# Splitting a batch of keys behind a tile's unpacking instead of ahead of it, with the copies and the store one step later

## The reference

```python
x   = x + xattn(layernorm(x), ctx)      # 1600 tokens, 5776 keys, 512 channels, 16 heads of 32
x   = x + ffn(layernorm(x))

q = quant(x @ Wq + bq) per head;  k = quant(ctx @ Wk + bk) per key and head;  v = quant(ctx @ Wv + bv) per column
attn = softmax(q @ k.T);  attn = round(attn / s) * s with s = max / 255
out  = (attn @ v) @ Wp + bp
```

## Time and profile before

| | before |
|---|---|
| median of 3 runs | 1861.85 us (1861.7 to 1870.55) |
| the profiled execution: its own time, its span | 1868.42 us, 1866.6 us |
| busy share of the span: PE, DVE, ACT, POOL | 88%, 91%, 75%, 76% |
| the 200 steps of attention | about 167 us to 1616 us of the span |
| chain of work that ended last, by engine | DVE 48%, PE 20%, POOL 12%, issue 9%, DMA 6%, ACT 4% |

### The profile page before, as it was taken

How to read it: one execution, slowest core, us unless ns; L and a number is a source line. 1 busy time by engine, 2 the same in 40 slices (tenths; PEclk the granted TensorE clock), 3 DMA queues, 4 the chain that set the end, 5 groups by cost and what they waited for, 6 DMA issues and landing times.

```text
span 1866.6 us, 42192 instructions
## 1 busy us (share of the span) xinstructions
PE 1638.0 (88%) x17032; PEld 1157.2 (62%) x17032; DVE 1694.2 (91%) x2665; ACT 1393.2 (75%) x1362; POOL 1422.8 (76%) x1153
## 2 busy tenths in 40 slices
PE   7997889988888888888888888888889888789998
PEld 6884666666555666655566666555555555467776
DVE  6868999999999999999999999999999999976665
ACT  2446889888988888989888988897788888732222
POOL 1432789989988899989888999898898898752232
PEclk9998999999999999989999999999999999889999
DMA  5677998999999998898998999789888998832221
GB/s 174 211 208 191 193 199 176 172 188 184 171 172 187 194 183 186 172 177 168 188 194 172 190 188 177 150 158 186 171 170 156 206 185 153 177 101 45 66 57 46
DMA packets 851533, 309.98 MB, mean 166 GB/s; under 512 B 784966, under 2 KB 813964, under 8 KB 851212
## 3 DMA queue, kind: packets, MB, share of 16 engines
q1 hardware_dynamic: 851340, 307.29, 80.8%
HBM read 74.26 MB, written 39.59 MB: 61 GB/s over the span
## 4 chain that ended last, share of the span: by engine, by line
DVE 48%; PE 20%; POOL 12%; issue 9%; DMA 6%; ACT 4%; SPq 1%; POOLq 0%; DVEq 0%; ACTq 0%
DVE S L1242 43%; POOL PT L1468 9%; PE PS L847 4%; DMA PP<-Pr 4%; PE PS L714 3%; ACT Pr L1054 2%; PE PS L682 2%; PE PK L884 2%; PE PK L655 2%; PE PK L657 2%; PE PO L657 1%; PE PO L655 1%; DMA XIT<-XI 1%; DVE MJ L1268 1%; PE PO L733 1%
## 5 line engine op out<-in xcount | busy, mean ns | idle before, releaser
L1242 DVE TENSOR_SCALAR_CACHE_REDUCE S<-PS,SQN 128x1536 f32<-128x1536 f32 (+1 forms) x768 | 1284.4, 1713 | 29.5 <-PE PS L714 23.3
L1468 POOL CAST PT<-PP 128x1536 uint16<-128x1536 uint8 (+1 forms) x800 | 1100.6, 1420 | 114.6 <-DMA PP<-Pr 112.6
L1054 ACT ACTIVATE Pr<-S,MS 128x5888 uint8<-128x5888 f32 x200 | 1041.2, 5206 | 171.4 <-DVE MJ L1268 141.9
L714 PE MATMUL PS<-KT,QT 96*128 96x512 bf16 (+1 forms) x2496 | 639.0, 376 | 133.2 <-DVE S L1242 120.2
L733 PEld LDWEIGHTS PO<-VI,PT 128*128 128x128 f16 x9200 | 339.9, 96 | 190.5 <-issue 23.3
L714 PEld LDWEIGHTS PS<-KT,QT 96*128 96x128 bf16 (+1 forms) x2496 | 199.5, 100 | 341.9 <-issue 133.5
L733 PE MATMUL PO<-VI,PT 128*128 128x32 bf16 x9200 | 356.7, 178 | 10.9 <-ACT AO L1008 5.5
L655 PE MATMUL PK<-WG,CT 128*128 128x128 f32 (+1 forms) x1288 | 215.0, 297 | 46.9 <-ACT VV L920 40.5
L657 PE MATMUL PK<-CT,WG 128*128 128x128 f32 (+1 forms) x1288 | 212.4, 294 | 0.0
L655 PEld LDWEIGHTS PK<-WG,CT 128*128 128x128 f32 (+1 forms) x1288 | 169.9, 195 | 53.9 <-issue 52.7
L657 PEld LDWEIGHTS PK<-CT,WG 128*128 128x128 f32 x1288 | 167.5, 193 | 1.7 <-issue 0.6
(11 more groups left out here) (151 smaller groups left out, 1563.0 us busy)
## 6 DMA issues: line engine op xcount, KB each, us to landing
CT<-ctxt SPq DMA_DIRECT2D x180, 256.0 KB, 3.2
k_rows<-KS SPq DMA_DIRECT2D x44, 512.0 KB, 4.0
q_rows<-QS SPq DMA_DIRECT2D x13, 512.0 KB, 4.3
W13F<-w13T SPq DMA_DIRECT2D x12, 352.0 KB, 3.5
PP<-Pr SPq DMA_TRANSPOSE x200, 6.0
XT<-x SPq DMA_DIRECT2D x12, 256.0 KB, 3.3
XR<-x SPq DMA_DIRECT2D x12, 256.0 KB, 3.4
base_rows<-XO SPq DMA_DIRECT2D x12, 256.0 KB, 3.4
```

The costliest lines, as they stand in the source:

```text
L714: last = pe.matmul(PS[n % 2][p0:p0 + r, f:f + w], QT[h % 3][0:PARTS * HD, q0:q0 + r], KT[h % 3][0:PARTS * HD, c * CHUNK + f:c * CHUNK + f ...
L1054: act.activation(Pr[i % 2].rearrange("p t q b -> p t b q"), S[i % 2].rearrange("p (t b q) -> p t b q", b=2, q=P), ACT.Exp, bias=MS[:, i % ...
L1242: v.tensor_scalar(S[i % 2][:, c * CHUNK:c * CHUNK + CW[c]], PS[n % 2][:, 0:CW[c]], neg_step, None, ALU.mult, ALU.min, accum_out=MN[:, i % ...
L1468: gp.tensor_copy(PT[i % 2][:, 2 * t0:2 * t1, :].rearrange("p (t b) q -> p t b q", b=2), PP[i % 2][:, t0:t1, :].bitcast(U8).rearrange("p t ...
```

## The change

`k_parts` of a batch moves on GpSimd from ahead of the unpacking of tile s to behind it (2.95 in place of 2). ScalarE's `k_high` moves from step s+2 to s+3, the store from step s+3 to s+4. The planner reads K_STORE as well, so it lays the pieces of heads anew.

```diff
-K_CAST, K_SPLIT, K_STORE = 1, 2, 3
+K_CAST, K_SPLIT, K_STORE = 1, 3, 4
@@ the list of GpSimd's work
-                    todo += [(step + 1, k_scale, (g, b)), (step + 2, k_parts, (g, b)),
+                    todo += [(step + 1, k_scale, (g, b)), (step + 2.95, k_parts, (g, b)),
                              (end + 5.95 + b * 2 / 3, v_quant, (g, b))]
```

## The result

The changed kernel takes 1869.66 us (median of 21 runs, 1862.54 to 1878.59), the kernel before in the same comparison 1863.81 us (21 runs, 1856.2 to 1871.96). The ratio is 1.0032, 95% interval 1.002 to 1.0044: **slower by 0.3%, some 6 us**. The forecast was 1858 and its range ended at 1868, so both the sign and the range missed. The kernel before had its median at 1861.85 us when the forecast was made and 2 us higher in this comparison; 1868 was 0.33% above the former, so the range ended at about the ratio that was measured. The sign is the larger miss.

What follows compares the result with a forecast made beforehand. VectorE bounds the kernel, busy 1400 of 1443 us from step 0 to 198. Terms 3.0 + 0.5 + 2 x 1.0 − 2 x 0.7 = 4.1 us saved, off the 1861.85 us median, gave 1858; range 1849 to 1868.

Steps and rivals of the forecast that it cites:

- The step that failed: Last batch of groups 1 and 2: its KS overwrite waits for the previous batch's store; 0.7 us lost each, bounds 0 and 2.8.
- Late copies cost nothing ahead of a conversion: ScalarE, seven g=1 batches three steps apart: copies right ahead of the next conversion cost nothing; bound 0.3 us each, 2 in all.
- Step 29: VectorE loses 3.52 us there; an earlier unpacking 22 and transpose 25 take back 3.0 us, bounds 0 and 3.5.
- The copies off steps 52 and 102: ScalarE's high-part copies leave steps where they delay the unit's copies PE awaits: 1.0 us gained each, bounds 0 and 1.5.
- The split out of the gap at (2,0): GpSimd's k_parts there leaves a gap, unpacking 51 starts 1.9 us later; costed at nothing, 1.9 at two places without cover.
- Exponential 131: ScalarE's exponential of tile 131 waited 1.62 us for its transpose; 0.5 us gained, bounds 0 and 1.
- The planner: Pieces of K move by a step or two; 1.5 to 2 us more for SP in some steps, hidden under waits.
- the slower one: Last batch's store lands late, unpackings 41 and 91 up to 4 us later, PE's clock drops again: 1871 us, chance 0.15.
- KD's wait: Sign: GpSimd's 67.1 us wait ahead of KD, for ScalarE's conversion, falls below 15 us.
- The wait ahead of KS: Sign: a new GpSimd wait of 2 to 4 us in batches (1,11) and (2,11), released by the store.
- The stretch: Sign: the attention part, steps 0 to 198, gets 4 us shorter while VectorE's busy time stays 1400 us.
- the group ends: Sign of being wrong: the stretches where a group ends, losing 8.6 and 6.0 us before, lose more than 11 and 9.

Runs made afterwards that it cites:

- the split alone: Kernel before with only GpSimd's k_parts moved behind the unpacking; copies, stores and planner as before: 1858.52 us, 0.9963, and again 1861.47 us, 1.0000.
- set 4: Four variants of late copies and stores on one chip, against the kernel before at 1862.22 us: 1865.8, 1863.84, 1861.87 and 1857.02 us.
- set 3: k_parts moved in all four, copies and stores early or late, planner old or new; kernel before 1862.03 us; ratios 1.0000, 1.0005, 1.0057, 1.0038.
- set 2: Four variants of late batches or new planner on one chip, against the kernel before at 1861.67 us: ratios 0.9986, 1.0020, 1.0026, 1.0029.

## Why the prediction was wrong

**The step that failed** is the last batch's: "That stretch is already led in part by SP's own queue, so not all of it counts; I take 0.7 each, bounds 0 and 2.8." The mechanism was there, at both places, with the store issued at 488.33 (488.2 to 489.5 forecast), KS free at 493.18 (491.2 to 493.5) and unpacking 41 at 493.73 (491.9 to 494.1). What was wrong is what that delay is worth. Only the tile's own path was followed, with the rest taken for covered by SP's queue. Behind the same wait stood the value's cast, whose buffer ScalarE needs ahead of an exponential. That path came last, and PE's clock was halved behind it, which the term did not count. Steps 39 to 47 and 89 to 97 grew by 4.6 and 6.3 us in the pair of profiles. Taking the wait away wins 6 to 7 us in the profiled executions and 2 to 5 by the ratios, where the forecast had 1.4 for both places and at most 5.6. Two experiments show that the wait at KS makes the stall: with batch 10 early, and with the last split later, the stretches are back at 63 to 64 us. That it travels by the value's cast is read from the trace: ScalarE's 2.92 us stand ahead of VQ, and what PE and VectorE wait for behind is ScalarE's. The unpackings follow close: PE could not have begun its product of step 46 more than 0.8 us sooner, since unpacking 42 ended at 505.78. Both experiments free both paths, so no run separates them, and neither path alone can be given the whole price.

**Late copies cost nothing ahead of a conversion** ("by the rows this costs nothing; bound 0.3 each, 2 in all") was wrong as well, within its bound. Steps 10, 20 and 30 each took 7.22 us and take 7.82, 7.83 and 7.71: 1.7 us together by the profiles; the medians can't show so little. They stay at 7.22 wherever those copies are early. ScalarE in the changed kernel at the first of them:

```profile
238.92 0.62 ACT L943 ACTIVATE KS<-KD 128x512 bf16<-128x512 bf16 x1
...
246.50 0.20 ACT L1004 ACTIVATE AO<-PO 128x32 f32<-128x32 f32 x1 [0.70 <-PE PO L733]
246.59 0.62 ACT L926 ACTIVATE KI<-KB 128x512 int8<-128x512 f32 x1
```

The copies stand at a step's end, the exponential behind them starts late, and the conversion of the next batch follows it. A step that is "just filled" has no room for 1.1 us more, whatever the one behind it has.

**Step 29** (3.0 forecast) measures 3.8 in the pair of profiles. But the kernel whose split had not moved takes 6.91 us there too, so the split is not needed for it: the new place of copies and store does it as well, and so does the split alone. Which link of the chain lets it go isn't separated. Whether the medians hold it is open: the split alone has step 29 short and stands at 1.0000 in one set and 0.9963 in another. The kernel before was profiled once, in an execution above its median; whether it loses those 3.5 us in every execution isn't settled. One program had step 29 at 6.92 us in one execution and at 8.01 in another. A term read from one execution was booked against the median in full.

**The copies off steps 52 and 102** (1.0 each) were right for the place; for the kernel no gain is shown. With the first batch's copies alone late, steps 48 to 57 and 98 to 107 take 75.4 and 75.6 us in set 4 against 77.4 and 77.8 for the split alone in set 3: 2.0 and 2.2 us less. But steps 58 to 88 take 227.6 us (229.8 in set 2) against 225.3, and steps 0 to 198 together are the same within a microsecond (1435.3 and 1434.7 against 1434.7 and 1434.6). The ratios agree: 0.9986 and 0.9971 with, 0.9963 and 1.0000 without, in other sets. In the changed kernel steps 58 to 88 are not longer (225.7 us), and its two stretches are 4 us shorter than before; how much of that is this term isn't separated.

**The split out of the gap at (2,0)**, costed at nothing: 0.9966 with the gap filled, 0.9971 without, in two sets. No cost is shown; one of 0.1% would not be seen.

**Exponential 131**: step 133 went from 7.42 to 6.85 us, 0.6 for the 0.5 forecast. Step 135 grew by as much (6.79 to 7.35), and not as its echo: with the split alone step 133 takes 6.86 us and step 135 6.79.

**The planner**, costed at nothing: with all batches late, as in the change, no cost shows (1444.9 and 1444.1 us against 1445.6 and 1444.4 in the last column; 1.0038 against 1.0057). With all early, both profiled executions are 7 us longer with the new planner, and the medians by 1.8 us in set 3. Why is open.

So of the ten microseconds between forecast (−4.1) and result (+5.9), some 1 to 5 are the last batch's wait, mis-sized, 1.7 the copies' pile-up, and up to 3 the gain of step 29, if the medians don't hold it. These are estimates from the profiles and ratios above. The rest is not tracked down: the runs of one kernel spread by 5 to 18 us.

**Of the rivals** it was the slower one, given 0.15, and its 1871 us is nearest. It had the drop of the clock behind the wait, which the forecast's own term had left out (0.96 before, 0.90 after in both stretches). It was held less likely because "this place's store took 3.0 us"; here KS came free 4.9 us behind the issue (488.33 to 493.18). Its condition, a delay of 2.8 us at unpacking 41, was not quite met: 2.4 us were enough (491.3 to 493.73).

**The signs** named ahead: KD's wait gone, transposes' wait at ScalarE down from 29.3 to 17.1 (about 20 forecast), step 29 under 7.8, VectorE's busy time unchanged: all true. The wait ahead of KS was to be 2 to 4 us and is 5.33. The stretch was to be 4 us shorter and is 1.5 longer. Of the signs of being wrong, one showed: a stall of step 29's size at another of the steps 28 to 60. Steps 45 and 46 took 14.5 us before and take 18.5. The other, the group ends losing more than 11 and 9 us, did not: over the steps of its two rows they lose 8.4 and 2.2, because in group 2 the new stall (steps 95 and 96) stands ahead of the row, which begins with step 97.

## What to carry to other kernels

When a change puts a wait into an engine whose order is written out, list everything queued behind it up to the next gap, and follow each item's buffer to the engine that needs it; the item with the least slack decides, and it need not be the one that the engine mainly works on. Look at the second item too: here it was 0.8 us behind the first. Where a store is made later, look for the next writer of its buffer first, at the place where the batches stand closest together, and move that writer behind work that others wait for. Before a term read from one execution is booked, ask whether other executions hold it. And when a stretch gets shorter, sum to the end: a stall can come back a few steps on.

## What was unexpected of the hardware

How much the drops of PE's clock can differ between executions of one program, and how much not. In steps 0 to 198 PE was granted half its clock for 71.7 us in the profile before and 81.9 after; a second execution of the changed kernel had 75.1. The split alone had 47.8 us both times, and with the new planner 64.9 and 75.1. The Trainium skill (TensorE: Matmul & The Clock Gate, Part 1: The HAM clock gate) has the clock follow how busy the engine was of late; by that rule, the trace agrees: the stall of step 46 came behind PE's wait of 2.08 us for ScalarE. Some drops sit where another execution of the same program has none. One kernel (late only if the next batch is four steps on) took 10.99 us for step 74 in one execution, at half clock, and 6.79 at full clock in the other. So one profile can carry several microseconds that its program does not owe: two of the eight pairs of the same program differ by 3.5 and 4.3 us over steps 0 to 198, the other six by 0.1 to 1.2.

And the same program can stand 0.24% and 0.37% apart in its ratio to the same kernel before, from one set to another (1.0029 and 1.0005; 0.9963 and 1.0000). Each 95% interval reaches only 0.12% to 0.19% to either side, and for the second program the two do not overlap. Differences under 0.3% are trusted here only where they came again.
